# A graph network on one core: setup, edges' slots and ranges' keys joined into one block, and its loads, clearing, round trips and masks moved between queues and engines

## The chip, the cores and the metric

The kernel runs on one core of a Trainium2 chip. The metric is the time of the whole program on the device in microseconds (us), from its first to its last instruction. The times are set beside one profiled execution, from which all rows below come.

The core has five engines that run their own instruction streams in order: TensorE (PE in the profile, PEld its weight loads), VectorE (DVE), ScalarE (ACT), GpSimd (POOL) and SyncE (SP). Transfers are issued by SP, ACT or POOL; the issue stands on a row of its own (SPq, ACTq), and the bytes are moved later by the core's DMA engines.

## What is computed

Four graph networks run one after the other over the same 3125 nodes of 64 features and the same 100,000 edges, which come sorted by destination. After each, its result is added to the nodes' rows and the sum is normalised:

```python
x = _layernorm(x + _L0_gnn_ref(x, src, dst, ...))                    # three attention layers
x = _layernorm(x + _L1_gnn_ref(x, edge_attr_64, ..., edge_index))    # an MLP on each edge, mean by destination
x = _layernorm(x + _L2_gnn_ref(x, edge_index, edge_type_8, ...))     # a weight matrix for each of 8 relations
x = _layernorm(x + _L3_gnn_ref(x, edge_index, edge_weight, ...))     # two rounds with weights split by sign
```

An attention layer needs, for each node, a softmax over its incoming edges; its first step is `z = h @ W.T + b` and two scores for each node.

## The kernel before

Before any layer runs, the kernel builds index structures from the edges. They are the subject here; the layers behind them are the same in both kernels.

1. `setup` (lines 245 to 296). SP loads the nodes (`x`) and 35 weights (36 transfers) and waits for all of them. GpSimd writes ramps and an identity, VectorE converts them and clears `big`, 128 x 3200 zeros.
2. `edge_slots` (311 to 506). Each edge gets a slot in the DRAM table `slots` by its source tile (25 of them) and destination bin. SP loads four arrays, 128 partitions of 784 edges each. VectorE works through one chain: tiles and bins by rounding (L384 to L396), columns of `meta` (L398 to L400), a running maximum (L402 on), 25 counts called tails (L426), and then the rank loop, which has three instructions for each of the 25 tiles: a mask `key == i + 1` (L441), a predicated copy of the previous tile's counts (L444) and a scan that counts along the edges (L448). ScalarE's stream begins with 60 transfers that clear `slots` from `big` (L355), and goes on with the first layer's `z` in seven batches (L361 to L366), each between two groups of matmuls on TensorE (L495, L501). Two small matmuls on TensorE stand around them: `ps_carry` (L491), on which the rank loop rests, ahead of the batches, and `ps_before`, `ps_all` (L505, L506), on which the last operations on VectorE rest, behind them.
3. `edge_keys` (567 to 663). SP loads three more arrays. VectorE reduces each tile's lowest and highest destination, SP sends these to DRAM and back to all partitions (`tile_ends`), VectorE computes which tiles each window of 25 nodes covers, and SP sends that to DRAM and back to one partition (`tile_ranges`, L616 and L619: two transfers of 125 rows of 4 bytes, and then one load).
4. `build_counts` (666 on) counts edges between nodes with one-hot products. Its TensorE stream takes `edge_attr` blocks that SP loads (L928). GpSimd waits for all 60 clearing transfers (`k.filled`) before it scatters its first record.

Each of the four is a block of its own: at its end all engines meet at a barrier, so none starts the next one earlier than the last has finished. VectorE's chains are built by `chain.link`, which makes it wait for each result:

```python
    def link(self, ins):
        self.n += 1
        ins.then_inc(self.sem, 1)
        self.eng.wait_ge(self.sem, self.n)
```

## Time and profile before

| | us |
|---|---|
| median of 3 runs (lowest, highest) | 3858.63 (3853.43, 3875.61) |
| the profiled execution's own time | 3875.63 |
| its span, first to last instruction | 3873.8 |
| VectorE's first operation of `build_counts` in it | 223.77 |

The profiled execution is at the upper end of the runs and 17 us above their median. The stretch that the change touches is the first 223.77 us of its span, 5.8% of it. A row of the timeline reads: start in us, duration in us, engine, line, operation, output<-input, and in brackets how long the engine sat idle before it and what it waited for.

### The profile page before, as it was taken

Reading aid. Unit: us, or ns where it says so; the run is one execution under the profiler, and the core shown is the slowest. Engines: PE = TensorE matmul, PEld = TensorE weight load, DVE = VectorE, ACT = ScalarE, POOL = GpSimd, SP = SyncE. Lnnn points to the kernel's source line nnn. Section 1 sums busy time; section 2 is a strip of 40 time slices with the busy share of each in tenths; the row PEclk is TensorE's granted clock in tenths of the full one; section 3 lists DMA queues with packets and bytes.
Section 4 is the critical chain, followed back from the end, with each engine's and each line's share of the span. In section 5 each row is a group of like instructions: output and inputs, shape, how many; then the busy total and the mean of one; then the engine's idle time right before and its main releaser. Section 6 shows DMA issues by size and latency. Waiting matters only on the chain. (4 is left out here: it accounts for less than half of the span.)

```text
span 3873.8 us, 77256 instructions
## 1 busy us (share of the span) xinstructions
PE 2866.3 (74%) x24985; PEld 2065.8 (53%) x25068; DVE 2910.3 (75%) x6871; ACT 1557.0 (40%) x3297; POOL 1498.4 (39%) x1395
## 2 busy tenths in 40 slices
PE   0158888887417707707769999699999699969994
PEld 0135555555302202202269999456565499959994
DVE  6877777777489999999977776555555588857876
ACT  0024444444204405405469999233333233322221
POOL 0035545444238737637600000155555134414441
PEclk9999889878659959959979999799999799989997
DMA  8936657465459828829846765122222144424441
GB/s 308 377 98 190 178 158 186 150 176 152 145 165 295 263 78 287 254 77 286 260 155 214 226 212 169 45 68 68 67 65 66 37 127 120 122 55 110 110 114 38
DMA packets 456800, 607.29 MB, mean 157 GB/s; under 512 B 87386, under 2 KB 339225, under 8 KB 456419
## 3 DMA queue, kind: packets, MB, share of 16 engines
q1 hardware_dynamic: 395623, 441.00, 38.6%
q0 software_dynamic: 43744, 87.66, 7.7%
q10 hardware_dynamic: 17052, 73.76, 4.9%
q8 instruction: 213, 3.49, 0.4%
q14 instruction: 168, 1.38, 0.1%
HBM read 364.05 MB, written 232.38 MB: 154 GB/s over the span
## 5 line engine op out<-in xcount | busy, mean ns | idle before, releaser
L915 POOL DMA_INDIRECT slots<-bc_rec,idx x400 | 392.1, 980 | 394.0 <-ACT bc_rec L875 291.2
L1214 PE MATMUL psum<-a_probs,z 128*65 128x512 f32 (+1 forms) x1050 | 436.3, 555 | 134.1 <-DVE a_probs L1112 130.7
L1851 DVE TENSOR_SCALAR rp_hot_dst<-rp_ramp,slot_key 128x696 bf16<-128x696 f16 x900 | 298.9, 401 | 231.7 <-PE psum L1995 228.5
L536 POOL DMA_INDIRECT slots<-h,idx x256 | 343.4, 1341 | 304.2 <-DMA h<-recs 232.9
L1148 ACT ACTIVATE a_tops<-a_tops,a_s_low 128x512 f32<-128x512 f32 (+2 forms) x300 | 283.0, 946 | 271.8 <-DVE a_tops L1103 256.3
L1828 POOL DMA_INDIRECT rp_fetch<-piece_rows,slot_row x283 | 278.5, 984 | 249.7 <-PE psum L1995 193.3
L1214 PEld LDWEIGHTS psum<-a_probs,z 128*65 128x65 f32 x1050 | 122.2, 139 | 443.8 <-DVE a_probs L1112 271.4
L1103 DVE SCALAR_TENSOR_TENSOR a_tops<-table,a_s_rest,big 128x512 f32<-128x512 f32 (+2 forms) x300 | 306.0, 1023 | 3.0 <-DMA big<-shift_rows 3.0
L1923 ACT ACTIVATE rp_msg<-psum 128x192 bf16<-128x192 f32 (+1 forms) x456 | 175.8, 386 | 312.2 <-PE psum L1969 275.6
L1112 DVE SCALAR_TENSOR_TENSOR a_probs<-a_tops,a_counts 128x512 f32<-128x512 f32 (+2 forms) x300 | 288.2, 962 | 10.5 <-ACT a_tops L1148 8.4
L794 PE MATMUL psum<-acc 128*128 128x512 f16 x1000 | 190.8, 338 | 106.4 <-issue 53.8
L1656 PE MATMUL psum<-sp_msg,sp_hot_dst 128*90 128x128 f32 x1800 | 261.4, 282 | 8.1 <-issue 7.1
L1656 PE MATMUL psum<-ep_msg,ep_hot_dst 128*90 128x131 f32 x1800 | 257.2, 278 | 3.4 <-ACT ep_msg L1562 2.9
L763 DVE TENSOR_SCALAR acc<-bc_ramp,bc_key_s,bc_base_s 128x625 f16<-128x625 f16 x500 | 242.0, 484 | 19.3 <-issue 18.9
L1656 PE MATMUL psum<-sq_msg,sq_hot_dst 128*90 128x128 f32 x1800 | 254.3, 278 | 1.8 <-issue 1.8
L1986 PE MATMUL psum<-rp_hot_dst,rp_msg 128*128 128x184 bf16 (+1 forms) x1151 | 240.2, 308 | 10.9 <-ACT rp_msg L1923 2.0
L1406 POOL DMA_INDIRECT sq_fetch<-far_rows,slot_row x148 | 151.4, 1023 | 169.7 <-ACT sq_msg L1593 160.5
L1205 PE MATMUL psum<-ident,a_shifts 128*10 128x128 f32 x15 | 5.7, 377 | 282.6 <-DVE a_shifts L1097 247.3
L1656 PEld LDWEIGHTS psum<-sp_msg,sp_hot_dst 128*90 128x90 f32 x1800 | 204.1, 159 | 12.9 <-issue 9.4
L1642 PE MATMUL psum<-edge_pieces,ep_hot_src 128*128 128x131 bf16 x2700 | 209.5, 222 | 1.6 <-ACT ep_hot_src L1577 1.5
L1656 PEld LDWEIGHTS psum<-ep_msg,ep_hot_dst 128*90 128x90 f32 x1800 | 206.5, 158 | 6.2 <-DVE ep_hot_dst L1442 5.6
L1464 DVE TENSOR_TENSOR ep_sums<-psum,ep_rec 128x393 f32<-128x393 f32 x300 | 169.8, 566 | 51.6 <-PE psum L1642 48.7
(456 smaller groups left out, 6978.4 us busy)
## 6 DMA issues: line engine op xcount, KB each, us to landing
slots<-big ACTq DMA_DIRECT2D x60, 1012.5 KB
ep_rec<-slots SPq DMA_DIRECT2D x60, 1012.5 KB, 6.2
a_counts<-edge_counts SPq DMA_DIRECT2D x75, 538.5 KB
a_counts<-edge_counts SPq DMA_DIRECT2D x150, 256.0 KB
a_counts<-edge_counts SPq DMA_DIRECT2D x75, 512.0 KB
edge_counts<-bc_counts SPq DMA_DIRECT2D x12, 3125.0 KB
hot_rows<-ep_hot_src SPq DMA_DIRECT2D x300, 96.0 KB
recs<-bc_rec SPq DMA_DIRECT2D x100, 270.0 KB
```

Of the source, the lines that this page charges most:

```text
L536: pool.indirect_dma_start(k.slots, bass.IndirectOffsetOnAxis(k.idx[:, at:at + 1], 0), self.rows[y][:, t, :], None).then_inc(self.scattered ...
L763: last = v.tensor_scalar(to_s[:, u, :], ramp[:, :], column(key_s, t), column(base_s, j), ALU.subtract, ALU.is_equal)
L915: pool.indirect_dma_start(k.slots, bass.IndirectOffsetOnAxis(k.idx[:, first + t:first + t + 1], 0), rec[:, j, t, :], None).then_inc(scatte ...
L1103: v.scalar_tensor_tensor(tops[:, cols], shift_1[:, cols], s_rest[:, s:s + 1], shift_2[:, cols], ALU.add, ALU.max).then_inc(topped, 1)
L1112: v.scalar_tensor_tensor(probs[:, cols], tops[:, cols], 1.0, counts[:, cols], ALU.min, ALU.mult)\
L1148: nc.scalar.activation(tops[:, cols], tops[:, cols], ACT.Exp, bias=s_low[:, s:s + 1])\
L1214: last = nc.tensor.matmul(sums[:, a:b], k.z[:, s, 0:D + 1], probs[:, a:b], start=s == 0, stop=True, skip_group_check=True)
L1642: last = nc.tensor.matmul(got[:, s, :], hot_src[:, c % HOT_SLOTS, s * P:(s + 1) * P], pieces[:, c % NT, piece, :], start=s == 0 and piece ...
L1656: last = nc.tensor.matmul(sum_bank(j)[:, s, :], hot_dst[:, c % DST_SLOTS, s, :], msg[:, c % MSG_SLOTS, s, :], start=i == 0 and s == 0, sto ...
L1828: pool.indirect_dma_start(fetch[:, n % FETCH_SLOTS, :], None, k.piece_rows, bass.IndirectOffsetOnAxis(k.slot_row[:, c:c + 1], 0))\
L1851: v.tensor_scalar(hot_dst[:, q % HOT_SLOTS, :], ramp[:, :], k.slot_key[:, q:q + 1], None, ALU.is_equal)\
L1986: nc.tensor.matmul(sum_bank(s, part), message(q)[:, 0:2 * D], hot_dst[:, q % HOT_SLOTS, a:b], start=starts_bank(q, part), stop=True, skip_ ...
```

## The change

The three blocks `setup`, `edge_slots` and `edge_keys` become one block in `edge_slots`, and tiles of `edge_keys` now live in memory that is free at that time (`k.table`, `k.acc`, `k.h`, and tiles of the rank section under second names).

- SP's queue: the edge arrays first, in the order in which VectorE uses them, then the nodes, the weights, and last the 60 clearing transfers. It waits for no load any more.
- ScalarE's queue: the round trips for `tile_ends` and `tile_ranges`. It waits in its stream for the first half of each before it issues the second. The clearing transfers leave it.
- ScalarE computes the two sign-split columns of `meta` and the 25 masks of the rank loop, each as a square and a rectifier: `relu(1 - (i + 1 - key)^2)`, in two buffers that the predicated copies free.
- VectorE: the parts of the old blocks follow each other, keys and ranges between the older parts of the rank section; the loop keeps two instructions for each tile.
- TensorE: `ps_carry` moves behind the seven batches of `z`.
- GpSimd writes the big ramp `all_rows` last.

```diff
             def _(sp):
+                sp.dma_start(dst_rows[:, :, :], d["dst_rows"]).then_inc(rows_in, 16)
+                sp.dma_start(plain_dst_i, d["dst"]).then_inc(keys_in, 16)
+                sp.dma_start(plain_src_i, d["src"]).then_inc(keys_in, 16)
                 sp.dma_start(dst_i[:, :], d["dst_rank"]).then_inc(loaded, 16)
...
+                sp.dma_start(k.x[:, :, :], d["x"].rearrange("(t p) f -> p t f", p=P)).then_inc(x_in, 16)
+                for to, source in parts:
+                    sp.dma_start(to, source).then_inc(weights_in, 16)
+                sp.wait_ge(cleared, 1)
...
-                    act.dma_start(to.rearrange("(p s) f -> p (s f)", p=P), flat[:, 0:per]).then_inc(k.filled, 16)
+                    sp.dma_start(to.rearrange("(p s) f -> p (s f)", p=P), flat[:, 0:per]).then_inc(k.filled, 16)
+
+            @block.scalar
+            def _(act):
+                act.wait_ge(ends_ready, 1)
+                act.dma_start(att.ends[0, :].rearrange("(p t) -> p t", t=7), low[:, :]).then_inc(ends_out, 16)
...
+                act.wait_ge(loaded, 4 * 16)
+                nc.scalar.activation(meta[:, 0:ET, 1], w[:, :], ACT.Relu).then_inc(marked, 1)
+                nc.scalar.activation(meta[:, 0:ET, 2], w[:, :], ACT.Relu, scale=-1.0).then_inc(marked, 1)
+                act.wait_ge(ranges_ready, 1)
+                for j in range(2):
+                    act.dma_start(att.ranges[j, :].rearrange("(p o) -> p o", o=1), ends[0:NWIN, 2 + j:3 + j])\
+                        .then_inc(ranges_out, 16)
+                act.wait_ge(ranges_out, 32)
+                act.dma_start(ranges[:, 0:2, :], att.ranges.rearrange("(o a) b -> o a b", o=1)).then_inc(ranges_in, 16)
                 for n, tiles in enumerate(batches):
...
+                act.wait_ge(numbers_made, 1)
+                act.wait_ge(tails_in, NT)
+                for i in range(NT):
+                    if i >= 2:
+                        act.wait_ge(chosen, i - 1)
+                    nc.scalar.activation(mask[:, i % 2, :], key[:, :], ACT.Square, bias=k.bin_lane[:, i:i + 1], scale=-1.0)\
+                        .then_inc(squared, 1)
+                    act.wait_ge(squared, i + 1)
+                    nc.scalar.activation(mask[:, i % 2, :], mask[:, i % 2, :], ACT.Relu, bias=k.ones[:, 0:1], scale=-1.0)\
+                        .then_inc(masked, 1)
...
                 v.tensor_scalar(diag[:, :], k.ident[:, :], top[:, 0:1], None, ALU.mult).then_inc(row_in, 1)
+                dve.wait_ge(weights_in, 16 * len(parts))
+                score_weights(k, chain, w_first, w_score, 0)
+                v.memset(x_turned[D:D + 1, :], 1.0).then_inc(w_made, 1)
...
                 for i in range(NT + 1):
-                    if i < NT:
-                        if i >= 2:
-                            dve.wait_ge(chosen, i - 1)
-                        v.tensor_scalar(mask[:, i % 2, :], key[:, :], i + 1.0, None, ALU.is_equal).then_inc(masked, 1)
...
-                pe.wait_ge(row_in, 4)
-                nc.tensor.matmul(ps_carry, link[:, :], tails[:, :], start=True, stop=True).then_inc(pe_done, 1)
+                pe.wait_ge(x_in, 16)
                 pe.wait_ge(w_made, 1)
...
                     last.then_inc(z_out, 1)
+                pe.wait_ge(row_in, 4)
+                nc.tensor.matmul(ps_carry, link[:, :], tails[:, :], start=True, stop=True).then_inc(pe_done, 1)
                 pe.wait_ge(row_in, 5)
```

This is how ScalarE's stream begins in the kernel before (`slots<-big` is the clearing, the rest is the first batches of `z`):

```order
L355 DMA slots<-big 128x2025 x60
L361 ACT_TABLE_LOAD
L361 ACTIVATE es_x_turned<-psum 64x512
L365 ACTIVATE z<-psum 128x264
L366 ACTIVATE d_low<-psum 128x4
```

And in the changed kernel:

```order
L330 DMA tile_ends<-es_low 112x7
L331 DMA tile_ends<-es_high 112x7
L333 DMA table<-tile_ends 128x784
L334 DMA table<-tile_ends 128x784
L336 ACT_TABLE_LOAD
L336 ACTIVATE meta<-es_w 128x784
L337 ACTIVATE meta<-es_w 128x784
L340 DMA tile_ranges<-es_ends 125x1 x2
L343 DMA es_ranges<-tile_ranges 1x250
L349 ACTIVATE es_x_turned<-psum 64x512
L353 ACTIVATE z<-psum 128x264
L354 ACTIVATE d_low<-psum 128x4
```

The 60 clearing transfers are gone from the head of the stream. Ahead of the first batch now stand the round trips, the first of which waits for VectorE's `es_low`, and a load that waits until `tile_ranges` has been written.

TensorE's stream in the kernel before, from its first matmul; L491 is `ps_carry`, L495 and L501 are the batches:

```order
L485 MATMUL psum<-ident,es_top 1x128
L487 MATMUL psum<-ones,es_row 128x1
L489 MATMUL psum<-es_diag,ones 128x128
L491 MATMUL psum<-es_tails,es_link 128x25
L495 MATMUL psum<-ident,x 64x128 x4
L501 MATMUL psum<-es_w_first,es_x_turned 128x67 x4
L495 MATMUL psum<-ident,x 64x128 x4
```

The same stream in the changed kernel, with the middle batches left out; L568 is `ps_carry`:

```order
L549 MATMUL psum<-ident,es_top 1x128
L551 MATMUL psum<-ones,es_row 128x1
L553 MATMUL psum<-es_diag,ones 128x128
L558 MATMUL psum<-ident,x 64x128 x4
L564 MATMUL psum<-es_w_first,es_x_turned 128x67 x4
...
L558 MATMUL psum<-ident,x 64x128
L564 MATMUL psum<-es_w_first,es_x_turned 128x67
L568 MATMUL psum<-es_tails,es_link 128x25
L570 MATMUL psum<-es_total,es_below 128x1
L571 MATMUL psum<-es_total,ones 128x1
```

`ps_carry` moved from ahead of the first batch to behind the last, and so behind all of ScalarE's work on the batches.

## Rows read from the trace of the kernel before

**Rows 1.** VectorE's timeline: each row behind a long wait, up to `build_counts`.

```profile
26.47 0.71 DVE L380 MEMSET es_ones<- 128x784 f32 x1 [20.03 <-PEq L126]
...
32.72 0.57 DVE L384 CAST es_dst<-es_dst_i 128x784 f32<-128x784 int32 x1 [3.29 <-DMA es_w<-in_weight_rank]
...
185.31 0.16 DVE L468 COPY es_before<-psum 128x1 f32<-128x1 f32 x1 [10.20 <-PE psum L506]
...
192.42 0.57 DVE L625 CAST ek_tile_no<-ek_tile_no_i 128x784 f32<-128x784 int32 x1 [2.72 <-POOL ek_base_i L599]
...
196.32 0.63 DVE L631 CAST ek_dst_rows_f<-ek_dst_rows 112x896 f32<-112x896 int32 x1 [2.56 <-DMA ek_src_i<-in_src]
...
222.26 0.28 DVE L662 SCALAR_TENSOR_TENSOR ek_row<-ek_row 1x125 f32<-1x125 f32 x1 [9.20 <-DMA ek_row<-tile_ranges]
...
223.77 0.23 DVE L767 CAST bc_ident<-ident 128x128 f16<-128x128 f32 x1 [0.99 <-PEq L126]
```

**Rows 2.** ScalarE's timeline: clearing transfers, first and last operation on `z`.

```profile
32.72 128.87 ACTq L355 DMA_DIRECT2D slots<-big  x60
...
162.91 0.59 ACT L361 ACTIVATE es_x_turned<-psum 64x512 f32<-64x512 f32 x1
...
184.61 0.17 ACT L366 ACTIVATE d_low<-psum 128x1 f32<-128x1 f32 x1
```

**Rows 3.** Windows: time, busy (count) by engine, clock, DMA share, GB/s.

```profile
33.00:34.00 1.00, 0.00 (x0) 0.00 (x0) 0.93 (x3) 0.00 (x0) 0.00 (x0) 1.00 0.51 211
...
183.00:184.00 1.00, 0.52 (x3) 0.24 (x2) 0.00 (x0) 0.60 (x3) 0.00 (x0) 1.00 0.54 219
```

**Rows 4.** DMA queues, 0 to 260 us: ScalarE's queue; packets, MB, share of 16 engines.

```profile
q10 hardware_dynamic: 8640, 62.21, 58.4%
```

**Rows 5.** SP's timeline: issue of the last two weights.

```profile
21.99 0.43 SPq L263 DMA_DIRECT2D w_b_3p<-in_L_gnn_b2p  x1
22.47 0.43 SPq L263 DMA_DIRECT2D w_b_3n<-in_L_gnn_b2n  x1
```

**Rows 6.** VectorE's timeline: sign-split columns, running maximum, first mask of the rank loop.

```profile
48.80 0.85 DVE L399 TENSOR_SCALAR meta<-es_w 128x784 f32<-128x784 f32 x1
50.22 1.76 DVE L402 TENSOR_TENSOR_SCAN es_top<-es_ones,es_d_bin 128x784 f32<-128x784 f32 x1
...
84.69 0.57 DVE L441 TENSOR_SCALAR es_mask<-es_key 128x784 f32<-128x784 f32 x1
```

**Rows 7.** VectorE's timeline: end of the rank loop.

```profile
159.49 1.02 DVE L444 COPY_PREDICATED es_rank<-es_mask,es_count 128x784 f32<-128x784 int32 x1
160.41 1.83 DVE L448 TENSOR_TENSOR_SCAN es_count<-es_same,es_carry,es_mask 128x784 f32<-128x784 f32 x1
162.27 1.03 DVE L444 COPY_PREDICATED es_rank<-es_mask,es_count 128x784 f32<-128x784 int32 x1
```

**Rows 8.** ScalarE's groups by shape: xcount | busy, mean ns | idle before.

```profile
L1148 ACT ACTIVATE a_tops<-a_tops,a_s_low 128x512 f32<-128x512 f32 x150 | 108.2, 721 | 105.0 <-DVE a_tops L1103 97.3 <-issue 7.6
...
L1148 ACT ACTIVATE a_tops<-a_tops,a_s_low 128x1024 f32<-128x1024 f32 x75 | 86.1, 1148 | 76.2 <-DVE a_tops L1103 71.2 <-issue 4.9
```

**Rows 9.** SP's timeline: the round trip of the ranges.

```profile
213.09 0.66 SPq L616 DMA_DIRECT2D tile_ranges<-ek_ends  x2
219.93 0.21 SPq L619 DMA_DIRECT2D ek_row<-tile_ranges  x1
```

**Rows 10.** ScalarE's timeline in the attention layers: write and dependent load, twice.

```profile
1123.37 0.30 ACTq L1167 DMA_DIRECT2D shift_rows<-a_shifts_t  x1
1128.70 0.33 ACTq L1171 DMA_DIRECT2D table<-shift_rows  x1
...
1427.59 0.30 ACTq L1167 DMA_DIRECT2D shift_rows<-a_shifts_t  x1
1428.85 0.33 ACTq L1171 DMA_DIRECT2D table<-shift_rows  x1
```

**Rows 11.** TensorE's timeline: first product of `build_counts` with loaded edge attributes.

```profile
231.66 2.05 PE L804 MATMUL psum<-w_W1a_edge,table 64*128 64x128 f32 x16
```

More of the change, by code:

```diff
@@ new lines, in _ @@
+                v.tensor_copy(tile_no[:, :], tile_no_i[:, :])
+                v.tensor_copy(keys.ramp[:, :], ramp_i[:, :])
+                v.tensor_copy(keys.base[:, :], base_i[:, :])
+                chain.link(v.tensor_copy(first_t[:, 0:1], first_t_i[:, :]))
+                v.tensor_scalar(first_t[:, 1:2], first_t[:, 0:1], WIN - 1.0, None, ALU.add)
+                v.memset(keys.s[:, ET:], -1.0)
+                v.memset(keys.t[:, ET:], -1.0)
+                dve.wait_ge(keys_in, 2 * 16)
+                plain_src, plain_dst, high_part, window = key, live, rank, last_key
@@ L383, in _ @@
+                magic_round(v, chain, window[:, :], plain_dst[:, :], 1.0 / WIN, -0.48)
+                chain.link(v.scalar_tensor_tensor(keys.s[:, 0:ET], window[:, :], float(COLS - WIN), keys.s[:, 0:ET],
+                                                  ALU.mult, ALU.add))
                 dve.wait_ge(loaded, 4 * 16)
```

242 lines of the change are left out of this document (94 added, 148 removed).

## The prediction, made before the changed kernel ran

> **What bounds the kernel now.** I read the timeline of VectorE from the start to `build_counts` first, because the three blocks hold one long chain on that engine, and looked only at what stands in brackets. Six waits there [rows 1] are 20.03 us (the barrier behind SP's weight loads), 3.29 (four edge arrays), 10.20 (`ps_all` from TensorE), 2.72 (barrier and ramps), 2.56 (three more arrays) and 9.20 (the ranges' way through DRAM): 48.00 us of 223.77. The rest, 175.77 us, is VectorE at work, its chained gaps and one barrier. So these blocks are bound by VectorE's chain, with holes.
>
> The 10.20 us have their cause on ScalarE. Its 60 clearing transfers occupy its stream from 32.72 for 128.87 us, `z` follows from 162.91 to 184.78 [rows 2], and TensorE has `ps_all` behind the last batch; VectorE goes on 0.53 us after ScalarE's last operation [rows 1, 2]. The loads and the clearing hang on the second resource, the DMA engines. From the middle of the window at 33 us to the middle of that at 183 us [rows 3] clearing takes 150.0 us for 62.21 MB [rows 4], 415 GB/s. That length isn't changed; only its start and what it stands ahead of are.
>
> Everything from `build_counts` on has the same instructions in both kernels and stands behind a barrier, so what the start of `build_counts` gains, the end gains, if no transfer is late there.
>
> **The change, part by part, on VectorE's chain.**
>
> *The waits.* With the arrays first in SP's queue each is wanted long after it lands. VectorE entered the old block at 26.47 and the four arrays were there at 32.72 [rows 1], 6.3 us later. Seven need at most twice that, about 12 us, of which the first three are wanted at 7 to 11 us and the last four at 19. The ends' round trip has from about 10 to 34 us. Nothing in this part is loaded by a barrier. If that cover failed, a late array would cost its lateness, at most the 3.29 of before. All six waits go: 48.00 us.
>
> *Work taken off.* The two columns of `meta` fill 48.80 to 50.22: 1.42 us [rows 6]. In the loop, the masks: before, it runs from 84.69 [rows 6] to 163.30, 78.61 us. What is left for a tile is visible at its end, where no mask stands between the scan and the copy: copy to scan 0.92, scan to copy 1.86 [rows 7], 2.78 together and 25 x 2.78 = 69.5, with the last copy's tail 69.6. That saves 9.0. So VectorE alone would reach `build_counts` at 223.77 - 48.00 - 1.42 - 9.0 = 165.35.
>
> *Do ScalarE's masks keep up?* The row nearest to them is the softmax's bias operation in SBUF, 721 ns for 512 columns and 1148 for 1024 [rows 8]: 0.834 ns a column, so 948 ns for 784, and 1.90 us for a square and a rectifier. A copy frees a buffer 1.02 after its start; the scan that needs the new mask starts 0.92 + 1.86 + 0.92 = 3.70 after the same start [rows 7]. That leaves 2.68 us for 1.90 and three handoffs; I cost it at nothing. Bounds: nothing, and the 9.0 again if a turn takes 3.4 us, since two tiles take a turn plus 2.88.
>
> *`ps_carry` behind the batches.* This is the new wait. Without it the loop would start at 78.0: the work before it is, each stretch from a row's start to where the next wait begins (its row's start less the wait): 26.47 - 20.03 = 6.44; 29.43 - 26.47 = 2.96; of the keys 193.76 - 192.42 = 1.34 and 213.06 - 196.32 = 16.74; and 84.69 - 32.72 less the 1.42, 50.55 [rows 1, 6]. `z` is now held by the ranges' first half. They are ready at 6.44 + 0.71 + 1.34 + 16.74 + (48.80 - 32.72) = 41.3. The write took 213.09 to 219.93, 6.84 us [rows 9], on DMA engines with nothing else to do; now the clearing is in flight, so call what it takes more c. ScalarE is free at 48.4 + c, the batches start at about 49.5 + c with TensorE's first group, end 21.9 later [rows 2] at 71.4 + c, and the first mask follows at 73.5 + c. ScalarE has nothing else queued that VectorE wants before. So 4.5 us of c are hidden, and beyond that each costs one.
>
> How large is c? A write of ten short rows and the load behind it are 1.26 us apart in the second layer and 5.33 in the first [rows 10], where other transfers were in flight: 4.1 more. The ranges are 2 x 125 rows of 4 bytes. A clearing packet takes 0.584 x 16 x 260 / 8640 = 0.281 us [rows 4]. If each of the 250 rows waits for one such packet and they spread over sixteen engines, that is 4.4 us more; on a single engine it would be 70. Below, c is nothing. I take 4.1 + 4.4 = 8.5, the middle of what the row supports: VectorE then arrives at 165.35 + 4.0 = 169.4.
>
> *Clearing in SP's queue.* The last weight's issue ended at 22.90 [rows 5]. Seven issues at the 0.48 that lie between its two rows go ahead of it, 3.4 us, so clearing is issued from 26.3, moves from 27.1 (0.8 after issue, as in [rows 2, 3]) and is through at 177.1. SP's own stream is done some 129 us after 26.3, at 155, so the barrier does not wait for it. But `build_counts`' attribute loads are in the same queue and follow the last clearing bytes: 177.1 + 1.3 = 178.4. TensorE wanted the first of them 7.9 us after the block's start [rows 1, 11], so a start before 170.5 only moves the wait. GpSimd's first scatter waits for clearing as well, to 177, and has its first record about 10 us after the start; that is hidden from 170 on.
>
> *Sum.* The start of `build_counts` that counts is the later of 169.4 and 170.5, and I add 1 for handoffs that have no row: 171.5. The gain is 223.8 - 171.5 = 52.3 us. On the profiled execution, 3875.6, that is 3823; it lay 17 us above the median. I put the gain on the median: 3858.6 - 52.3 = 3806.
>
> **The rivals.**
>
> *A: the ranges' small writes take turns with clearing on few engines.* 125 rows divide by five, not by sixteen. On five engines each has 50 of them, 50 x 0.281 = 14.1, c = 18.2, and `build_counts` starts at 165.35 + 13.7 = 179.1. The gain is 44.7, the time 3814. For it: the same write took 6.84 us even alone [rows 9], five times the quiet one of [rows 10], so it isn't spread well. Against: nothing shows strict turns. The Trainium skill (DMA: Bandwidth & Descriptors, Queues, rings and completion order) states that each engine goes round the queues packet by packet, and (same page, Why a DMA increments its semaphore by 16 and not by 1) that 125 rows would be given to five engines. No row before shows either for this transfer.
>
> *B: ScalarE's masks set the loop's pace.* The turn is 3.4 us or more. For it: three handoffs and two in-order operations; against: 0.78 us of room. Up to 9 us on 165.35 + 4, less what the 170.5 hides: 3812 and more with A.
>
> *C, slower: the round trip starves.* If the ranges' write is served only when clearing has drained, ScalarE is free at 178, the batches end at 201, the first mask is there at 203, and 87.3 us of VectorE's chain follow (78.0 to 165.35): `build_counts` at 290, 66.5 us later than before, 3925. It decides from a write that lands later than 111 us, c of 63. Against: in [rows 10] a write beside other transfers took 5.33 us, not tens.
>
> *D: given back.* The earlier start is eaten in `build_counts` or later, by a transfer that now collides. For it: records are scattered at once behind clearing. Against: the queues are empty at 178, as they were at 184 before.
>
> *E: better than forecast.* c stays under 4.5 and TensorE's wait for attributes is absorbed by slack in `build_counts`: start at 165.4, gain 58.4, 3800.
>
> **How the numbers follow.** Chances: forecast 0.55, A 0.20, E 0.10, B 0.07, C 0.04, D 0.04. The likeliest is 3806, its own range 3797 to 3816. Runs of the kernel before lie from 5 us below to 17 above their median. From E's 3800, less 10, to A's and B's 3815, plus 13: 3790 to 3828; left out are C, D and outliers in the runs. About 0.5% (19 us) is what a measurement of this kernel can tell from no change. A, B, E and the forecast are beyond it: faster 0.92. D is within: 0.04. C is slower: 0.04.
>
> **What would show it.** In the profile of the changed kernel: VectorE without a wait above 1 us until the rank loop; the loop's copies 2.8 us apart; the loop's first scan at 78 to 83 us (92 under A, after 200 under C); the two issues of `tile_ranges` at about 41 and the load behind them at 50 to 58; ScalarE's mask operations at 0.95 us each; full DMA from 27 to 177 us; VectorE's first operation of `build_counts` at 169 to 172, and TensorE's wait for attributes at about 178. The prediction is wrong if the ranges' load comes later than 70, if the loop's period is above 3, if clearing ends later than 185, or if `build_counts` lasts longer than it did.

## The result, and the profile of the changed kernel

| | before | after |
|---|---|---|
| median of the runs | 3863.18 us (4 runs, 3853.43 to 3875.61) | 3824.77 us (4 runs, 3819.35 to 3828.30) |
| profiled execution: time, span | 3875.63, 3873.8 us | 3828.30, 3826.3 us |
| first operation of `build_counts` on VectorE | 223.77 | 179.94 |
| first product with loaded edge attributes on TensorE | 231.66 | 194.98 |

The ratio is 0.9905 (95% interval 0.9883 to 0.9927): 38.4 us or 0.95% faster. The forecast was 52.3 us and 3806; the measured time is inside the range of 3790 to 3828 and outside the likeliest case's own 3797 to 3816. Two runs behind this document, one of the kernel before (4228.07 us) and one of experiment 8 (5898.34), fell in a slower state of the chip and stand in none of its medians. I read the start again, engine by engine.

Behind its first operation VectorE's timeline shows no wait over 1 us until the row at 90.12; the first column is the start, the second the duration.

```profile
4.49 2.63 DVE L396 CAST bin_lane<-es_ints 128x90 f32<-128x90 int32 x1
4.55 2.59 DVE L397 CAST es_bins_f<-es_bins 128x36 f32<-128x36 int32 x1
...
90.12 0.18 DVE L498 COPY es_carry<-psum 128x25 f32<-128x25 f32 x1 [12.20 <-PE psum L568]
...
91.97 1.85 DVE L508 TENSOR_TENSOR_SCAN es_count<-es_same,es_carry,es_mask 128x784 f32<-128x784 f32 x1 [0.73 <-ACT es_mask L363]
93.86 1.03 DVE L504 COPY_PREDICATED es_rank<-es_mask,es_count 128x784 f32<-128x784 int32 x1
94.78 1.84 DVE L508 TENSOR_TENSOR_SCAN es_count<-es_same,es_carry,es_mask 128x784 f32<-128x784 f32 x1
...
160.93 1.03 DVE L504 COPY_PREDICATED es_rank<-es_mask,es_count 128x784 f32<-128x784 int32 x1
...
179.94 0.23 DVE L740 CAST bc_ident<-ident 128x128 f16<-128x128 f32 x1 [1.18 <-PEq L126]
```

The six waits of [rows 1], 48.00 us, are gone, and one of 12.20 us has come. The loop's 25 copies are 2.79 us apart on average, from 93.86 to 160.93. The views behind this one show where the new wait is from. First ScalarE's timeline, of which the first two rows are the write of the ranges and the load behind it (6.84 us apart in [rows 9], now 24.81), the third the first turn of x, and the last two the first tile's mask.

```profile
43.11 1.56 ACTq L340 DMA_DIRECT2D tile_ranges<-es_ends  x2
67.92 0.22 ACTq L343 DMA_DIRECT2D es_ranges<-tile_ranges  x1
68.19 0.59 ACT L349 ACTIVATE es_x_turned<-psum 64x512 f32<-64x512 f32 x1 [47.26 <-DMA tile_ranges<-es_ends]
...
89.94 0.95 ACT L360 ACTIVATE es_mask<-es_key,bin_lane 128x784 f32<-128x784 f32 x1
90.92 0.95 ACT L363 ACTIVATE es_mask<-es_mask,ones 128x784 f32<-128x784 f32 x1
```

SP's timeline: the transfer right behind x, the last weight's issue, the clearing, and the first attribute loads.

```profile
5.17 7.11 SPq L319 DMA_DIRECT2D w_W<-in_L_gnn_W  x1
...
34.64 0.43 SPq L319 DMA_DIRECT2D w_b_3n<-in_L_gnn_b2n  x1
35.12 134.13 SPq L325 DMA_DIRECT2D slots<-big  x60
179.90 4.55 SPq L901 DMA_DIRECT2D table<-in_edge_attr  x5
```

Windows of the first core: after the busy times come TensorE's granted clock, the DMA engines' share and GB/s.

```profile
43.00:68.00 25.00, 2.78 (x9) 1.61 (x9) 23.03 (x52) 0.00 (x0) 0.00 (x0) 1.00 1.02 343
68.00:100.00 32.00, 17.37 (x73) 14.27 (x73) 18.66 (x32) 14.06 (x29) 0.00 (x0) 1.00 1.01 418
...
193.00:194.00 1.00, 0.00 (x0) 0.00 (x0) 0.61 (x3) 0.00 (x0) 0.00 (x0) 0.50 0.84 182
```

GpSimd's timeline, its first scatter; it has to wait until the slots are cleared.

```profile
194.77 1.16 POOL L880 DMA_INDIRECT slots<-zero_rec,zero_idx  x1 [187.72 <-DMA slots<-big]
```

TensorE's timeline, the row that answers to [rows 11].

```profile
194.98 3.78 PE L777 MATMUL psum<-w_W1a_edge,table 64*128 64x128 f32 x16 [6.92 <-DMA table<-in_edge_attr]
```

The reader is to see two separate delays. While the ranges' 250 rows are written, ScalarE stands still and `z` is late, so VectorE waits. In the same 25 us the clearing moves 343 GB/s instead of 418, and it began at 35.12 and not at 26.3. It is through just before 194.77, and the attribute rows behind it in the same queue reach TensorE at 194.98, 15.04 us after VectorE had started the block. Between the start of `build_counts` and this product lay 7.9 us before. So the shift that counts is that of the product, 231.66 - 194.98 = 36.7 us, not the 43.8 of VectorE's start. The rest of the kernel keeps it: the medians are 38.4 us apart. ScalarE's table load at the start of the attention layers went from 1029.35 to 988.23, 41.1 us, but single executions scatter there: two later traces of the same changed kernel have it at 988.79 and 1000.51.

### The profile page after: what moved, and what is told of

It reads as the page before. It is cut to its first block and busy times, and to the rows that moved or that the text cites. A ratio compares the mean times of both kernels' runs of the same rounds, so it can differ in the third digit from the quotient of the medians.

```text
span 3826.3 us, 77315 instructions
## 1 busy us (share of the span) xinstructions
PE 2883.1 (75%) x25068; PEld 2074.3 (54%) x25068; DVE 2900.4 (76%) x6844; ACT 1609.5 (42%) x3349; POOL 1499.4 (39%) x1395
## 5 line engine op out<-in xcount | busy, mean ns | idle before, releaser
L1085 DVE SCALAR_TENSOR_TENSOR a_probs<-a_tops,a_counts 128x512 f32<-128x512 f32 (+2 forms) x300 | 289.3, 965 | 10.7 <-ACT a_tops L1121 7.2
L1959 PE MATMUL psum<-rp_hot_dst,rp_msg 128*128 128x512 bf16 x1234 | 258.2, 313 | 6.2 <-ACT rp_msg L1896 1.9
L736 DVE TENSOR_SCALAR acc<-keys_ramp,keys_s,keys_base 128x625 f16<-128x625 f16 x500 | 243.8, 488 | 3.2 <-issue 3.1
L1629 PEld LDWEIGHTS psum<-sp_msg,sp_hot_dst 128*90 128x90 f32 x1800 | 204.5, 160 | 11.4 <-issue 9.5
```

What stands on the lines that cost most here:

```text
L736: last = v.tensor_scalar(to_s[:, u, :], ramp[:, :], column(key_s, t), column(base_s, j), ALU.subtract, ALU.is_equal)
L1085: v.scalar_tensor_tensor(probs[:, cols], tops[:, cols], 1.0, counts[:, cols], ALU.min, ALU.mult)\
L1629: last = nc.tensor.matmul(sum_bank(j)[:, s, :], hot_dst[:, c % DST_SLOTS, s, :], msg[:, c % MSG_SLOTS, s, :], start=i == 0 and s == 0, sto ...
L1959: nc.tensor.matmul(sum_bank(s, part), message(q)[:, 0:2 * D], hot_dst[:, q % HOT_SLOTS, a:b], start=starts_bank(q, part), stop=True, skip_ ...
```

## The experiments

Two theories. **Theory 1**: two chains end at the first attribute product. One is VectorE's (start of `build_counts` plus 7.9 us), the other the clearing's (its drain, then the attribute rows behind it in SP's queue). The later one sets the time; in the changed kernel that is the clearing's, and what VectorE's gains alone is absorbed. **Theory 2**: only VectorE's chain counts, so removing its 12.2 us wait brings 12 us. The clearing's end is read from GpSimd's first scatter, which waits for it. A second question goes along: why the ranges' write takes 24.8 us.

The runs came from three jobs, each with runs of the kernel before in between: the first four kernels on a chip where it took 3680.11 us (11 runs), the next four beside 3876.29 (18), the last four beside 3862.19 (17). Times are compared within a job only; the first of them had no run of the changed kernel itself. The places in the first 240 us hardly differ between executions of the same code (first product of the changed kernel at 194.98, 196.21 and 195.85).

### 1. The ranges' load is waited for later

ScalarE issues the write, makes `z` and all masks, and only then waits for the write and loads the ranges.

```diff
-                act.wait_ge(ranges_out, 32)
-                act.dma_start(ranges[:, 0:2, :], att.ranges.rearrange("(o a) b -> o a b", o=1)).then_inc(ranges_in, 16)
                 for n, tiles in enumerate(batches):
...
                 for i in range(NT):
...
+                act.wait_ge(ranges_out, 32)
+                act.dma_start(ranges[:, 0:2, :], att.ranges.rearrange("(o a) b -> o a b", o=1)).then_inc(ranges_in, 16)
```

> The ranges' write is issued as in the changed kernel, but ScalarE waits for it, and issues the load behind it, only after the rank loop's masks, so no part of z waits for it. Theory 1 (two limits: ScalarE held by the write, and behind it clearing's drain, to which TensorE's first attribute product at 195.0 us is tied): VectorE's wait of 12.2 us before the rank loop goes, its first operation of build_counts comes at 167 instead of 179.9, but the first attribute product stays at 193 to 195 and the attention layers start at 985 to 988 instead of 988.2: the time is 0 to 4 us lower than the changed kernel's. Theory 2 (the chain on VectorE alone sets the gain, clearing's drain is absorbed): the attention layers start at 975 and the time is 13 us lower.

VectorE's timeline of this run:

```profile
78.63 0.19 DVE L498 COPY es_carry<-psum 128x25 f32<-128x25 f32 x1 [0.77 <-PE psum L568]
79.79 1.85 DVE L508 TENSOR_TENSOR_SCAN es_count<-es_same,es_carry,es_mask 128x784 f32<-128x784 f32 x1
```

GpSimd's, and TensorE's:

```profile
192.90 1.17 POOL L880 DMA_INDIRECT slots<-zero_rec,zero_idx  x1 [185.85 <-DMA slots<-big]
```

```profile
193.21 3.78 PE L777 MATMUL psum<-w_W1a_edge,table 64*128 64x128 f32 x16 [16.81 <-DMA table<-in_edge_attr]
```

The wait is gone and `build_counts` starts at 168.29, 11.65 us earlier than in the changed kernel. But the clearing still passes 43 to 68 us at 342 GB/s, GpSimd's first scatter is at 192.90, and TensorE has waited 16.81 us when the first product comes at 193.21. Time 3641.20, ratio 0.9891 (0.9876 to 0.9906). That is 5 us from the changed kernel's 0.9905 in another job, with an interval that holds both nothing and 12. What speaks against Theory 2 stands inside the job: experiment 4's block starts 18.7 us later than this one, but its first product comes only 1.25 us later, its table load at the start of the attention layers 0.5 later (835.52 and 835.00), and its median is 4.5 longer, with intervals of 5 to 6 us either side. Theory 2 would have all of the 18.7 at the end. It falls here. The expectation's 985 to 988 for that table load was a place of the first chip.

### 2. The ranges' write in 128 rows

The packet counts fit a write of 125 rows by five DMA engines: of queue 10's 260 packets 250 are rows and 10, two for each of five engines, are not. With 128 rows all sixteen would take part.

```diff
-                    act.dma_start(att.ranges[j, :].rearrange("(p o) -> p o", o=1), ends[0:NWIN, 2 + j:3 + j])\
+                    act.dma_start(att.ranges[j, :].rearrange("(p o) -> p o", o=1), ends[:, 2 + j:3 + j])\
...
-                act.dma_start(ranges[:, 0:2, :], att.ranges.rearrange("(o a) b -> o a b", o=1)).then_inc(ranges_in, 16)
+                act.dma_start(ranges[:, 0:2, :], att.ranges[:, 0:NWIN].rearrange("(o a) b -> o a b", o=1)).then_inc(ranges_in, 16)
...
-        self.ranges = nc.dram_tensor("tile_ranges", (2, NWIN), FP32, kind="Internal").ap()
+        self.ranges = nc.dram_tensor("tile_ranges", (2, P), FP32, kind="Internal").ap()
```

> The ranges are written as 128 rows of 4 bytes instead of 125, nothing else. Theory 1 with few engines (125 rows lie on five DMA engines, where each waits for a clearing packet; 128 would lie on sixteen): the write and the wait for it fall from 24.8 us to 7 to 12 us, VectorE's wait before the rank loop goes from 12.2 to 0 to 2, clearing ends 3 to 4 us earlier since no five engines are held, the first attribute product at 190 to 191, the time 3 to 5 us lower than the changed kernel's. Rival (the write is slow because its rows share lines of DRAM, or because it waits behind a queue of clearing on every engine): it stays at 20 us or more and nothing moves.

ScalarE's timeline of this run:

```profile
43.05 1.60 ACTq L340 DMA_DIRECT2D tile_ranges<-es_ends  x2
64.31 1.16 ACTq L343 DMA_DIRECT2D es_ranges<-tile_ranges  x1
```

Its windows:

```profile
43.00:68.00 25.00, 4.62 (x18) 3.46 (x19) 23.03 (x52) 0.59 (x1) 0.00 (x0) 1.00 1.03 241
50.00:55.00 5.00, 1.03 (x4) 0.54 (x4) 4.83 (x8) 0.00 (x0) 0.00 (x0) 1.00 1.21 107
```

21.3 us in place of 24.8, and not the 7 to 12 expected, although the rows are now spread three times as wide (288 packets, 256 and 2 x 16). The clearing suffers more: 241 GB/s over those 25 us, first scatter at 198.06, 5.2 later than in experiment 1. So the count of rows for one engine does not set the write's length by itself. VectorE's start is 2.7 earlier than in the changed kernel; the time, 3644.37, ratio 0.9907 (0.9893 to 0.9921), shows no gain.

### 3. The first eight attribute loads on ScalarE's queue

At the start of `build_counts` ScalarE issues them, and SP no longer does, so they don't stand behind the last clearing bytes.

```diff
+                for j in REC_ORDER:
+                    act.dma_start(attr[j], k.dram["edge_attr_64"][:, j * BATCH * P:(j + 1) * BATCH * P]).then_inc(attr_in[j], 16)
...
-                for j in REC_ORDER:
-                    load_attr(0, j)
```

> The first eight attribute loads of build_counts are issued from ScalarE's queue instead of SP's, where clearing is still queued. Theory 1: TensorE's wait of 6.9 us in front of the first attribute product goes, it comes at 188 instead of 195.0, GpSimd still scatters from 195 on, and the attention layers start 3 to 7 us earlier (981 to 985). Theory 2 (that wait is absorbed later anyway): within 1 us of 988.2.

`build_counts` starts at 181.03 and TensorE's first product is at 188.95, 7.92 later, without a wait:

```profile
188.95 2.37 PE L777 MATMUL psum<-w_W1a_edge,table 64*128 64x128 f32 x16
```

GpSimd's first scatter stays at 194.17, since it waits for the clearing itself. Time 3640.71, ratio 0.9897 (0.9884 to 0.9910). So the product's wait was the queue's order. The attention layers' table load is at 827.91, 7.1 before experiment 1's, near the 3 to 7 of Theory 1, but the two medians, 0.5 us apart, don't tell them apart. Whether the scatter that still waits for the clearing holds up what follows is not shown.

### 4. The masks back on VectorE

ScalarE's loop goes, and VectorE's rank loop makes each mask itself, as before.

```diff
-                    nc.scalar.activation(mask[:, i % 2, :], key[:, :], ACT.Square, bias=k.bin_lane[:, i:i + 1], scale=-1.0)\
...
-                    nc.scalar.activation(mask[:, i % 2, :], mask[:, i % 2, :], ACT.Relu, bias=k.ones[:, 0:1], scale=-1.0)\
...
+                        v.tensor_scalar(mask[:, i % 2, :], key[:, :], i + 1.0, None, ALU.is_equal).then_inc(masked, 1)
```

> The 25 masks go back to VectorE, everything else as in the changed kernel. The loop's period goes from 2.79 to 3.13 us and build_counts starts at 188 instead of 179.9. Theory 1 (clearing's drain is the last limit): the first attribute product comes at 196 instead of 195.0 and the time is 1 to 3 us higher. Theory 2 (VectorE's chain sets the gain): 8 us higher.

The loop's period is 3.13 us again and `build_counts` starts at 187.01, 7.1 later than in the changed kernel:

```profile
187.01 0.23 DVE L734 CAST bc_ident<-ident 128x128 f16<-128x128 f32 x1 [1.19 <-PEq L126]
```

GpSimd's and TensorE's timelines:

```profile
190.59 1.55 POOL L874 DMA_INDIRECT slots<-zero_rec,zero_idx  x1 [183.54 <-DMA slots<-big]
```

```profile
194.46 2.05 PE L771 MATMUL psum<-w_W1a_edge,table 64*128 64x128 f32 x16
```

The first product comes the floor of 7.45 behind the start, without a wait: here VectorE's chain sets it, and the clearing was through 3.9 us before (issued at 32.77, first scatter at 190.59). It is not later than in the changed kernel's own trace, 194.98. Time 3645.65, ratio 0.9907 (0.9892 to 0.9921), 4.5 us over experiment 1's. So of what the masks free on VectorE most is absorbed, as the two chains end within 4 us of each other without them; what they bring to the time lies within the scatter of the runs.

### 5. The changed kernel as a control

Nothing is edited.

> The changed kernel itself, as the control of its neighbours. Both theories: ratio to the kernel before 0.988 to 0.993; VectorE's wait for the carries of some 12 us, first instruction of build_counts near 180, clearing issued near 33 to 35 and landed some 134 us later as far as it delays the first transfers behind it, first attribute product near 195.

3840.04 us, ratio 0.9904 (0.9884 to 0.9924); wait for the carries 13.25, start 181.00, first scatter 195.99, first product 196.21. The gain of the change holds on a second occasion.

### 6. The ranges turned by TensorE

ScalarE no longer writes and loads them; two products with the identity put them into PSUM, and VectorE copies them out.

```diff
-                    act.dma_start(att.ranges[j, :].rearrange("(p o) -> p o", o=1), ends[0:NWIN, 2 + j:3 + j])\
...
-                act.dma_start(ranges[:, 0:2, :], att.ranges.rearrange("(o a) b -> o a b", o=1)).then_inc(ranges_in, 16)
...
+                pe.wait_ge(ranges_ready, 1)
+                for j in range(2):
+                    last = nc.tensor.matmul(ps_ranges[:, j, 0:NWIN], ends[:, 2 + j:3 + j], k.ident[:, 0:NWIN], start=True, stop=True)
+                last.then_inc(ranges_in, 1)
...
+                dve.wait_ge(ranges_in, 1)
+                chain.link(v.tensor_copy(ranges[:, 0:2, :], ps_ranges[:, :, 0:NWIN]))
```

> The ranges' ends no longer go through DRAM: TensorE turns the two columns by two small products and VectorE copies them out of PSUM, so ScalarE has no small write and no load before the turns of z. Both theories: VectorE's 12 us wait goes (0 to 2 us left), build_counts starts near 168; the clearing, which no longer runs beside 250 small rows, loses no 4 to 5 us between 43 and 68 and drains near 190. Theory 1 (the drain of the clearing is what the first attribute product waits for, so VectorE's lead is absorbed): first attribute product near 190, time 4 to 5 us under the control's. Theory 2 (what VectorE's chain gains arrives at the end): 12 us under the control's.

Its windows, and below them GpSimd's timeline:

```profile
43.00:68.00 25.00, 16.52 (x68) 12.59 (x68) 22.95 (x53) 4.77 (x13) 0.00 (x0) 1.00 1.01 417
```

```profile
188.57 1.16 POOL L880 DMA_INDIRECT slots<-zero_rec,zero_idx  x1 [181.52 <-DMA slots<-big]
```

In the places Theory 1 is right: no wait, start at 168.26, clearing at 417 GB/s throughout, first product at 189.10, 7.1 us before the control's. The time is 3841.89 (ratio 0.9900, 0.9875 to 0.9924), 1.9 over the control's: neither theory's number. The intervals are some 9 us wide on either side, so 7 us less are not excluded, but 12 hardly fit. GpSimd's scatters, counted through `build_counts`, are 7 to 9 us ahead of the control's up to the fortieth, 1.5 ahead at the hundredth and 4 behind at the three hundredth; the code there is the same. So in this trace the lead is lost inside `build_counts`; its table load of the attention layers is at 996.64, between those of the two controls (988.79 and 1000.51). The mean granted clock of its six runs is 0.890 and of the control's six 0.892. Within the kernel before's runs a clock lower by 0.001 goes with a time longer by some 2 us (0.898 with 3870.86, 0.888 with 3893.21), so this clock, if it is a cause, would account for about 5 us of the 9 missing. More on it below.

### 7. The clearing early, the other weights on ScalarE's queue

SP issues the seven arrays, the first layer's five weights, x and the clearing; ScalarE issues the other 31 behind the sign-split columns.

```diff
+                for to, source in parts[:FIRST_PARTS]:
+                    sp.dma_start(to, source).then_inc(weights_in, 16)
+                sp.dma_start(k.x[:, :, :], d["x"].rearrange("(t p) f -> p t f", p=P)).then_inc(x_in, 16)
...
+                for to, source in parts[FIRST_PARTS:]:
+                    act.dma_start(to, source).then_inc(rest_in, 16)
```

> Only the five weights of the first layer and x stand ahead of the clearing on SP's queue; the other 31 weight transfers go out on ScalarE's. The ranges still go through DRAM, so VectorE starts build_counts near 180 as in the control. Theory 1: the clearing is issued at 14 to 18 and drained near 170 to 178, so the first attribute product comes 7.9 us behind build_counts' start, near 188, and the time is 3 to 8 us under the control's. Theory 2: VectorE's chain is as long as in the control, so within 1 us of the control's.

This one missed in the other direction. ScalarE's timeline:

```profile
19.27 1.18 ACTq L343 DMA_DIRECT2D w_W<-in_L_gnn_W  x1
...
67.99 1.02 ACTq L343 DMA_DIRECT2D w_b_3n<-in_L_gnn_b2n  x1
69.05 13.16 ACTq L346 DMA_DIRECT2D tile_ranges<-es_ends  x2
117.38 0.22 ACTq L349 DMA_DIRECT2D es_ranges<-tile_ranges  x1
```

Beside the clearing, issued from 7.75, the 31 weight transfers take 1.0 to 2.3 us each to issue and hold ScalarE from 19 to 69; the ranges' write comes behind them and takes 48.3 us. `build_counts` starts at 229.51, first product at 237.50, time 3880.74, ratio 1.0008 (0.9992 to 1.0025). That is rival C's mechanism in part: 25.9 us from the later issue (69.05 against 43.12) and 22.5 from the longer write (48.3 against the control's 25.8) are 48.4, and `build_counts` starts 48.5 later than in the control. It also shows the other side of both theories: VectorE's chain is later than the clearing here, and the time is longer by as much, +40.7 against the control with the product +41.3.

### 8. The clearing only behind the ranges' write

SP waits ahead of the clearing until the ranges have landed in DRAM.

```diff
+                sp.wait_ge(ranges_out, 32)
```

> SP starts the clearing only once the write of the ranges has landed. If the 24.8 us between the write's issue and the load's are contention with the clearing's packets, they fall to 7 to 9 us (6.84 before), VectorE's wait for the carries goes to 0 to 2 us and build_counts starts near 168; if they belong to ScalarE's queue itself, they stay over 20 us. Theory 1: the clearing, issued near 50, drains near 185 to 200 plus what it waits in the queue, so the first attribute product comes near 200 to 208 and the time is 3 to 10 us over the control's. Theory 2: 10 to 12 us under the control's.

ScalarE's timeline:

```profile
43.12 0.81 ACTq L341 DMA_DIRECT2D tile_ranges<-es_ends  x2
49.97 0.22 ACTq L344 DMA_DIRECT2D es_ranges<-tile_ranges  x1
```

The same write on the same queue takes 6.85 us when the clearing is held back, as in [rows 9]. The 18 us more are contention with the clearing's packets. VectorE's wait for the carries falls to 0.77. It then stands 13.85 us at the barrier, which I had not reckoned with: SP's issue of the clearing lasts until 179.40.

```profile
180.50 0.23 DVE L741 CAST bc_ident<-ident 128x128 f16<-128x128 f32 x1 [13.85 <-PEq L126]
```

First scatter 203.93, first product 204.54, time 3859.86, ratio 0.9950 (0.9931 to 0.9968), 19.8 over the control's. Theory 1's 3 to 10 us are too few; the product alone is 8.3 later. The mean clock of its runs, 0.8895, may hold some 6 us of the rest; about 5 stay unexplained.

### 9. The control again

Nothing is edited; it stands beside the three kernels that follow.

> The changed kernel itself again, as the control of its neighbours on this chip. Both theories: ratio to the kernel before 0.988 to 0.993, first attribute product near 195.

3830.79 us, ratio 0.9918 (0.9886 to 0.9950). First product 195.85.

### 10. The clearing first, all else on SP's queue

The clearing stands directly behind the five weights of the first layer and x; the other 31 weights go behind 41 of the 60 clearing transfers. The ranges still pass through DRAM.

```diff
                 for c in range(0, NCHUNK, FILL):
...
+                    if c == 40 * FILL:
+                        for to, source in parts[FIRST_PARTS:]:
+                            sp.dma_start(to, source).then_inc(rest_in, 16)
+                sp.wait_ge(rest_in, 16 * (len(parts) - FIRST_PARTS))
```

> The early clearing alone, without the fault of the kernel that moved 31 weight transfers to ScalarE's queue: the same order on SP's queue as in the kernel with both, the ranges still through DRAM. The write of the ranges stands at 43 beside the clearing again: 21 to 26 us to the load's issue, VectorE waits 10 to 13 us for the carries, build_counts starts at 178 to 182. Theory 1: clearing drained at 172 to 180, first attribute product near 188 (7.9 us behind the start), time 5 to 8 us under the control's. Theory 2: within 1 us of the control's. Should the write take 36 us or more, as beside the weights on ScalarE's queue, the clearing's packets alone slow it, and the time is over the control's.

SP's timeline:

```profile
7.42 91.73 SPq L329 DMA_DIRECT2D slots<-big  x41
99.19 6.34 SPq L332 DMA_DIRECT2D w_W<-in_L_gnn_W  x1
...
136.71 26.36 SPq L329 DMA_DIRECT2D slots<-big  x19
```

TensorE's:

```profile
188.00 3.88 PE L785 MATMUL psum<-w_W1a_edge,table 64*128 64x128 f32 x16
```

The ranges' write takes 24.49 us, VectorE waits 11.88, the block starts at 179.60 and the first product follows 8.4 later without a wait. The clearing's end is at 187.9 and not at 172 to 180: in the 37 us from 99 to 136 the weights' small packets leave the DMA engines partly idle (100 to 150 us: share 0.85, 323 GB/s). Both chains now end together. Time 3812.31, ratio 0.9883 (0.9845 to 0.9921), 18.5 under the control's by the medians, where the product's shift is 7.9. By the ratios it is 13 us (0.9883 against 0.9918), and the two intervals overlap widely: neither 8 us nor no gain at all is excluded.

### 11. Both

The edit of 6 and that of 10 together:

```diff
-                act.dma_start(ranges[:, 0:2, :], att.ranges.rearrange("(o a) b -> o a b", o=1)).then_inc(ranges_in, 16)
...
+                    if c == 40 * FILL:
+                        for to, source in parts[FIRST_PARTS:]:
+                            sp.dma_start(to, source).then_inc(rest_in, 16)
```

> Both ends at once: the ranges' ends are turned by TensorE and go through no DRAM, and on SP's queue the clearing stands directly behind the loads, the first layer's five weights and x, with the other 31 weight transfers behind 41 of its 60 transfers; ScalarE's queue gets nothing new. Clearing issued from 7.8, drained at 165 to 176 (60 x 1.037 MB at 415 GB/s are 150 us); build_counts starts at 167 to 169; first attribute product 7.9 us later, near 176, with no wait for its rows over 3 us. Theory 1 (the later of the clearing's drain and VectorE's chain sets the end): 16 to 20 us under the control's time, ratio 0.985 to 0.987. Theory 2 (only VectorE's chain counts): 12 us under it. If part is given back by a lower granted clock, as the 0.890 of the run with turned ranges beside 0.892 of its control suggests, 8 to 14 us.

GpSimd's timeline:

```profile
183.07 1.16 POOL L888 DMA_INDIRECT slots<-zero_rec,zero_idx  x1 [176.02 <-DMA slots<-big]
```

Start 168.15, first product 183.86 behind a wait of 7.48; I had put it at 176. The clearing is late by the weights in its middle again, and is again the later chain. Time 3819.43, ratio 0.9896 (0.9867 to 0.9926), 11.4 under the control's, product 12.0 earlier. That lies in the 8 to 14 us named for the case with the lower clock, and under Theory 1's 16 to 20, which rested on a product at 176; by the intervals none of these is excluded.

### 12. The kernel before with the clearing on SP's queue

In `edge_slots` the 60 transfers are issued by SP behind the four array loads and no longer by ScalarE.

```diff
-                    act.dma_start(to.rearrange("(p s) f -> p (s f)", p=P), flat[:, 0:per]).then_inc(k.filled, 16)
...
+                    sp.dma_start(to.rearrange("(p s) f -> p (s f)", p=P), flat[:, 0:per]).then_inc(k.filled, 16)
```

> The kernel before with one part of the change alone: in the block of the edges' slots the 60 clearing transfers are issued from SP's queue, so ScalarE's two sign columns no longer stand behind their issue. VectorE's wait of 10.2 us at the end of that block goes, the clearing drains as before (near 191, before the block of the ranges' keys). Expected: first instruction of build_counts at 213 to 215 instead of 223.8, time 9 to 11 us under the kernel before, ratio 0.997 to 0.9975. If the wait is only put off (the next small round trips stand behind the clearing's packets for longer): within 4 us of the kernel before.

VectorE's timeline:

```profile
35.26 0.57 DVE L383 CAST es_dst<-es_dst_i 128x784 f32<-128x784 int32 x1 [5.63 <-DMA es_w<-in_weight_rank]
...
216.19 0.23 DVE L766 CAST bc_ident<-ident 128x128 f16<-128x128 f32 x1 [0.99 <-PEq L126]
```

The 10.20 us of [rows 1] are gone: that wait was ScalarE's stream behind the 60 issues, as read. 2.54 come back at the front, since the clearing now starts while its block's arrays are loading and the last of them lands later (35.26 against 32.72). 7.6 us are left at the start of `build_counts`, 7.8 at the product. Time 3849.75, ratio 0.9968 (0.9945 to 0.9992), 12.4 under the kernel before.

### All runs side by side

Shift against the kernel before of VectorE's start of `build_counts` and of the first attribute product, each from one trace; of the median time in the same job; and the mean granted clock of the runs less that of the kernel before's.

| run | start | product | time | clock |
|---|---|---|---|---|
| 1, later wait | -55.5 | -38.5 | -38.9 | -0.003 |
| 2, 128 rows | -46.5 | -33.2 | -35.7 | 0.000 |
| 3, attributes on ScalarE's queue | -42.7 | -42.7 | -39.4 | -0.001 |
| 4, masks back | -36.8 | -37.2 | -34.5 | -0.001 |
| 5, control | -42.8 | -35.5 | -36.3 | -0.001 |
| 6, ranges by TensorE | -55.5 | -42.6 | -34.4 | -0.003 |
| 7, weights on ScalarE's queue | +5.7 | +5.8 | +4.5 | 0.000 |
| 8, clearing behind the write | -43.3 | -27.1 | -16.4 | -0.003 |
| 9, control | -43.5 | -35.8 | -31.4 | -0.004 |
| 10, clearing first | -44.2 | -43.7 | -49.9 | 0.000 |
| 11, both | -55.6 | -47.8 | -42.8 | -0.004 |
| 12, before, clearing on SP | -7.6 | -7.8 | -12.4 | 0.000 |

The time follows the product: ten of twelve are within 6.2 us, the others 8.2 and 10.7. From VectorE's start it is off by 11 to 27 us in six of them. On the slower chips the largest misses to the long side (6, 8, 9, 11) are all runs with a clock lower by 0.003 to 0.004. In these TensorE also stood still for more than 7 us before its first attribute product, which the kernel before and runs 7, 10 and 12 don't have. But run 2 stood still for 13 us and run 5 for 7.1 without the lower clock, run 1 on the faster chip has both the lower clock and a stand of 16.8 us and no miss, and runs 5 and 9 are the same code, so that wait alone doesn't settle it. What does is open.

## Why the prediction came out as it did

**Right.** The six waits go. ScalarE's masks take 0.95 us (0.948 forecast) and keep up; the loop's copies are 2.79 apart (2.78). SP's stream is done before the barrier. The gain at the first product, 36.7 us, is there at the end (38.4), and the time is faster by more than 0.5%.

**The step that failed: how large is c.** The term was 8.5 us, "the middle of what the row supports"; it measured 24.81 - 6.84 = 18.0. With the 4.5 hidden, VectorE would pay 13.5 instead of 4.0; experiment 1 measures 11.65. Rival A gave c as 18.2 and the start as 179.1; it is 179.94. Its number is right. Its mechanism, one turn per row on five engines, is not shown: by the same rule sixteen engines would take 6.84 + 4.4 = 11.2 us, and experiment 2 took 21.3. The Trainium skill (DMA: Bandwidth & Descriptors, Why a DMA increments its semaphore by 16 and not by 1) gives five engines for 125 rows, and the 260 packets agree; the trace of the kernel before has the same 260 for this write, so that trace did bear on it. Its rule that an engine goes round its queues packet by packet (same page, Queues, rings and completion order) isn't enough here to give the time: a packet is there typically 9 to 17 descriptors, where the prediction counted one row against one row of the clearing. Experiment 8 shows that all of c is contention: 6.85 us with the clearing held back. What sets its size stays open. A short row beside the clearing costs about (21.3 - 6.85) / 16 = 0.9 us for a row where an engine has sixteen, against 18.0 / 50 = 0.36 where it has fifty; no single price per row fits both.

**The step that failed second: when the clearing is through.** I had 177.1 for it and 178.4 for the rows behind it; they were 194.77 and 194.98. Three parts make up the 17.7 us. Its issue began 8.8 us late (35.12 for 26.3): I priced seven more issues at 0.48 each, but the one right behind x stood 7.11 us where in the old order it had stood 2.71, and three more took 1.69 to 2.00 while ScalarE's broadcast loads ran. The ranges' write took from the clearing 159.65 - 154.25 = 5.4 us, by the stretch from the clearing's first issue to GpSimd's first scatter here and in experiment 6 (the other traces with this write have 157.8 to 161.5, experiment 8 without it 153.9). The remaining 3.4 is that stretch without any write, 154.25, against the 150.8 of the sum. Contention was costed on the side of the small write only, and it works both ways. The prediction had named this as a sign against itself: the clearing ends later than 185. A second of its signs came too, by little: `build_counts` lasted 808.3 us from VectorE's first operation to the next table load, where it had lasted 805.6. That is less than single executions of the changed kernel differ there.

**How they combine.** I used "the later of two" rightly, but with both ends near 170 the choice seemed free of risk. With the clearing's end at 195 it decides. The prediction's start "that counts" was 171.5; the product less the floor of 7.9 gives 187.1, 15.6 later, and 52.3 - 15.6 = 36.7 stand beside the measured 38.4.

**Why the range held.** The time itself is 18.4 over the forecast's 3806.3: 13.9 are the gain, and the rest is that the kernel before measured 3863.18 and not 3858.63. That 3824.77 lies inside the range was in part luck. The range reached to 3828 for rivals A and B and the scatter of the runs; no rival had a clearing that ends 17.7 us late, and the time came out near A's forecast with room for scatter, by another path.

**What was small.** On VectorE's side everything but c was small: experiment 1, without the wait, starts at 168.29 where 165.35 and 1 for handoffs were reckoned. 1.8 of these 1.9 are two conversions at the start that took 2.6 us instead of 0.2: the operation behind them starts at 7.18 and no longer at 5.35.

**The rivals.** A is the one that happened, in VectorE's numbers; without its wait the first product came only 1.8 us earlier (experiment 1). B is refuted: 0.73 us once, then 2.8 a tile. C is refuted for this kernel; in experiment 7, where the small write took 48 us and landed past C's 111, it occurred in part. D is not seen in the medians of the changed kernel. E needed a small c.

## What to carry to other kernels

When a long transfer is moved, price the small transfers beside it and the long one itself, both ways; the round trip of 250 short rows took 18 us longer than alone and 5.4 from the clearing. Where two chains meet at one instruction, write down each one's arrival there, and follow that instruction rather than the start of its block. Order a queue by when things are needed, but keep the big transfer's start early: the order here put 36 weight transfers ahead of the clearing, of which five belong to the first layer, whose `z` is made in this block. The version with the clearing first (3812.31, control 3830.79 in the same job) has the lowest median of its job, though neither the control nor the one with both edits (3819.43) is apart from it by more than the runs scatter; its first product is 7.9 us earlier than the control's.

## What the runs showed of the hardware

- The write of 2 x 125 rows of 4 bytes took 6.85 us alone, 23.9 to 25.9 beside the clearing on another queue, and 48.3 with 31 weight transfers ahead of it on its own queue as well. In 128 rows it took 21.3 and slowed the clearing to 107 GB/s for 5 us, where 415 are usual.
- From first clearing issue to the first scatter: 154.25 and 153.91 us undisturbed (experiments 6 and 8), 157.82 to 161.49 beside the write in 125 rows (the changed kernel, its two controls, experiments 1, 3 and 4), 164.93 beside that in 128.
- Small transfers in the middle of the clearing, in its own queue, let the engines run partly idle: with 31 weight transfers there the rate was 331 GB/s over 50 us, where it had been 417 (experiment 11).
- The issue of the transfer right behind the load of x stood 7.11 us (6.71 to 7.50 in the other traces with this order). In experiment 10, where the first clearing transfer stands there and the weights go ahead of x, it was the clearing's that stood, 7.07 us.
- Beside GpSimd's 2.88 us iota into `all_rows` (4.17 to 7.05), two small conversions from integers on VectorE took 2.63 and 2.59 us; the same shapes took 0.20 and 0.17 before, when they ran later than the iotas. That the iota is the cause was not tried alone.
- TensorE's granted clock was 0.50, its 1.2 GHz level, at 193 us after the wait for the attribute rows, and the same sixteen products took 3.78 us instead of 2.05 [rows 11].
